# Differential attention with a mixture of experts on one core: the sums of a quad copied by ScalarE, multiplied by GpSimd and transposed once

## The reference, cut to what matters

```
scores = einsum('bhqd,bhkd->bhqk', q, k)
probs = softmax(scores)                       # 32 half heads, in pairs (1, 2)
w = probs[:, :, 0] - lam * probs[:, :, 1]
attn = einsum('bhqk,bhkd->bhqd', w, v)
attn = attn * rsqrt(mean(attn * attn) + EPS) * subln_g
```

## Time and profile before

| what | value |
|---|---|
| median of 3 runs | 6056.91 us (6054.91 to 6063.63) |
| profiled execution | 6064.04 us, span 6062.2 us |
| mean granted TensorE clock | 0.970 |
| PE busy | 5630.7 us (93%) |
| DVE busy | 5537.9 us (91%) |
| ACT busy | 4845.1 us (80%) |
| POOL busy | 2006.0 us (33%) |
| maxima, line 691 | 4096, 4671.1 us busy |
| exponentials, line 677 | 8192, 4368.8 us busy |
| transposes of the sums, line 703 | 256, 179.2 us busy |
| transposes of the output, line 708 | 128, 54.0 us busy |

### The profile page before, as it was taken

The page is one execution under the profiler, slowest core; times in us unless marked ns, Lnnn a source line. Parts: engine busy times, 40 slices in busy tenths (PEclk is TensorE's granted clock), DMA queues, the critical chain, the costliest instruction groups (busy, mean ns, idle before and its releaser), DMA issues. The chain is left out here.

```text
span 6062.2 us, 166095 instructions
## 1 busy us (share of the span) xinstructions
PE 5630.7 (93%) x50896; PEld 2015.1 (33%) x50896; DVE 5537.9 (91%) x6200; ACT 4845.1 (80%) x8950; POOL 2006.0 (33%) x3781
## 2 busy tenths in 40 slices
PE   8878999999999999999999999999999999987775
PEld 4542233333333333333333333333233323325424
DVE  7868999999999999999999999999999999967706
ACT  5755888888888888889888888888888888873304
POOL 7981222222222222222222222222222222225406
PEclk9997999999999999999999999999999999998877
DMA  5672222222232222222222222222222222216598
GB/s 178 203 202 49 49 52 52 51 52 52 52 52 51 52 51 52 51 50 52 52 47 51 52 51 48 51 51 51 50 52 52 52 52 51 52 35 199 173 359 272
DMA packets 436840, 493.13 MB, mean 81 GB/s; under 512 B 99283, under 2 KB 298099, under 8 KB 436195
## 3 DMA queue, kind: packets, MB, share of 16 engines
q1 hardware_dynamic: 435171, 483.57, 32.7%
q10 hardware_dynamic: 1024, 0.53, 0.0%
HBM read 360.60 MB, written 123.21 MB: 80 GB/s over the span
## 5 line engine op out<-in xcount | busy, mean ns | idle before, releaser
L677 ACT ACTIVATE at_e<-at_ps_e 128x512 f32<-128x512 f32 x8192 | 4368.8, 595 | 542.5 <-PE at_ps_e L766 373.2
L691 DVE TENSOR_REDUCE at_largest<-at_ps_m 128x1 f32<-128x1024 f32 x4096 | 4671.1, 1202 | 56.2 <-PE at_ps_m L795 53.0
L782 PE MATMUL at_ps_o<-at_e,at_v 128*32 128x256 f32 (+1 forms) x30720 | 2687.1, 422 | 12.3 <-issue 8.2
L795 PE MATMUL at_ps_m<-k_stack,q_stack 48*128 48x512 bf16 x8192 | 2500.1, 385 | 132.7 <-DVE at_largest L691 58.3
L766 PE MATMUL at_ps_e<-q_stack,k_stack 51*128 51x512 bf16 x8192 | 2505.7, 383 | 5.2 <-issue 2.3
L782 PEld LDWEIGHTS at_ps_o<-at_e,at_v 128*32 128x32 f32 x30720 | 845.0, 149 | 1567.3 <-issue 935.0
L766 PEld LDWEIGHTS at_ps_e<-q_stack,k_stack 51*128 51x128 bf16 x8192 | 598.1, 93 | 1678.3 <-ACT at_e L677 1641.0
L596 POOL TENSOR_TENSOR at_negated<-at_zeros,at_largest_t 128x32 f32<-128x32 f32 x256 | 64.7, 253 | 3262.7 <-DVE at_largest_t L698 3262.7
L795 PEld LDWEIGHTS at_ps_m<-k_stack,q_stack 48*128 48x128 bf16 x8192 | 607.6, 93 | 203.5 <-DVE at_largest L691 172.2
L639 POOL TENSOR_TENSOR at_rms<-at_mean_eps,at_minus_half 128x16 f32<-128x16 f32 x128 | 372.7, 2912 | 10.0
L436 PE MATMUL pr_ps_q<-pr_xn_t,pr_w 128*128 128x512 f32 x512 | 232.3, 596 | 2.0 <-issue 1.3
(11 more groups left out here) (130 smaller groups left out, 2856.0 us busy)
## 6 DMA issues: line engine op xcount, KB each, us to landing
k_stack<-k_parts SPq DMA_DIRECT2D x1536, 64.0 KB
q_stack<-q_parts SPq DMA_DIRECT2D x256, 192.0 KB
q_stack<-q_parts SPq DMA_DIRECT2D x256, 128.0 KB
w_first<-in_w SPq DMA_DIRECT2D x32, 1024.0 KB, 11.7
ex_w_second<-in_w SPq DMA_DIRECT2D x32, 1024.0 KB, 12.7
q_parts<-pr_parts SPq DMA_DIRECT2D x96, 256.0 KB, 2.4
k_parts<-pr_parts SPq DMA_DIRECT2D x96, 256.0 KB, 2.8
pr_x_in<-in_x SPq DMA_DIRECT2D x16, 1024.0 KB, 5.8
```

The source lines that it names most:

```text
L677: nc.scalar.activation(e[:, j % E_BUFS], ps_e[:, bank(u, j)], ACT.Exp, scale=SCALE).then_inc(exp_done, 1)
L691: nc.vector.reduce_max(largest[:, u % 2, j // SIDE, j % SIDE:j % SIDE + 1], ps_m[:, j % 2], AX.X).then_inc(max_done, 1)
L782: last = nc.tensor.matmul(ps_o[32 * tile:32 * tile + 32, columns], v[:, u, tile // 2, kt::TILES], e[:, (QUAD * g + tile) % E_BUFS, columns ...
L795: last = nc.tensor.matmul(ps_m[:, j % 2, half * HALF:(half + 1) * HALF], q_stack[rows, u, pair, c, t * P:(t + 1) * P], k_stack[rows, u, pa ...
```

## The change

The sums no longer go through DVE out of PSUM. ACT copies `ps_o` into SBUF (`sums[:, c]`), and sets `sums_read`. The copy of c stands behind the exponential of position 6 of the following eight periods (`COPY_AT` = 7). The column order of the weights differs between the parts: for c = 0 v first and then ones, for c = 1 ones first and then v. So POOL can multiply the two copies element by element, and the product `crossed` holds V1 s2 in 16 rows and V2 s1 in the other 16. The product s1 s2, needed for EPS, would be spread badly by this; it is made from `totals`, into which SP moves one row of the sums for each of the four head halves and each c, with eight small DMAs for each quad. DVE then transposes both products at once, 544 columns, at g = 5 (`turn_sums`), and the output at g = 11 instead of g = 7 (`turn_out`). `finish` on POOL starts with the two products, waits for the transpose, and then needs fewer steps of its own. The loop of DVE now starts at g = 12.

On SP the order is new: `load_rows` of c = 1, the four totals of c = 1, then `load_stacks`, then `load_rows` of c = 0, `load_v`, the four totals of c = 0, and the store of the quad before.

```
-                        load_rows(n + AHEAD, (u + AHEAD) % BUFS, 1)
...
+                def move_totals(n, c):
+                    sp.wait_ge(sums_read, 2 * n + c + 1 + 1)
+                    sp.sem_inc(passed, 1)
+                    sp.wait_ge(crossed_done, 2 * n + 2)
+                    for g in range(QUAD):
+                        row = 32 * g + (0 if c else VD)
+                        sp.dma_start(totals[32 * g:32 * g + BLOCKS, c], sums[row:row + 1, c]).then_inc(totals_moved, 16)
...
+                    pool.wait_ge(sums_read, 2 * n + 2 + 1)
+                    if not (isinstance(n, int) and n == 0):
+                        pool.wait_ge(sums_turned, n)
+                    nc.gpsimd.tensor_tensor(crossed[:, 0:HALF], sums[:, 0], sums[:, 1], ALU.mult).then_inc(crossed_done, 1)
+                    pool.wait_ge(totals_moved, 16 * TOTAL_DMAS * (n + 1))
+                    nc.gpsimd.tensor_tensor(crossed[:, HALF:], totals[:, 0], totals[:, 1], ALU.mult).then_inc(crossed_done, 1)
+                    pool.wait_ge(sums_turned, n + 1)
...
+                def copy_sums(n, c):
+                    act.wait_ge(sums_done, GROUPS * n + TILES * (c + 1) + E_GROUPS)
+                    act.wait_ge(crossed_done, 2 * n + 2)
+                    nc.scalar.copy(sums[:, c], ps_o[:]).then_inc(sums_read, 1)
+                def turn(n, u, last):
+                    exponentials(n, u, COPY_AT, HALVES // 2 + COPY_AT)
+                    copy_sums(n, 0)
+                    exponentials(n, u, HALVES // 2 + COPY_AT, HALVES)
+                    if not last:
+                        exponentials(n + 1, (u + 1) % BUFS, 0, COPY_AT)
+                    copy_sums(n, 1)
...
-                    nc.vector.transpose(sums_t[:, c].rearrange("p b d -> p (b d)"), ps_o[:]).then_inc(sums_read, 1)
+                    dve.wait_ge(crossed_done, 2 * (n + 1) + 2)
+                    nc.vector.transpose(crossed_t[:], crossed[:]).then_inc(sums_turned, 1)
...
-                    if g == LAG - 1 and last_quad:
-                        turn_sums(n - 1, 1)
-                    if g == HEAD - 1 and last_quad:
+                    if g == TURN_SUMS and last_quad:
+                        turn_sums(n - 1)
+                    if g == TURN_OUT and last_quad:
                         turn_out(n - 1, u - 1)
-                    if g == TILES + LAG - 1 and this_quad:
-                        turn_sums(n, 0)
```

More of the change, by code:

```diff
@@ L492, in attend @@
             parts = sb("parts", [P, PARTS, BLK], BF16)
-            sums_t = sb("sums_t", [P, 2, BLOCKS, BLK])
-            scaled_s1, both = sb("scaled_s1", [P, BLOCKS]), sb("both", [P, BLOCKS])
-            normed, attn_t = sb("normed", [P, 2, BLOCKS, VD]), sb("attn_t", [P, BLOCKS // 2, 2, VD])
+            sums, totals = sb("sums", [P, 2, HALF]), sb("totals", [P, 2, BLK])
+            crossed, crossed_t = sb("crossed", [P, HALF + BLK]), sb("crossed_t", [P, HALF + BLK])
+            second, both = sb("second", [P, BLOCKS, VD]), sb("both", [P, BLOCKS])
+            attn_t = sb("attn_t", [P, BLOCKS // 2, 2, VD])
             attn, square = sb("attn", [P, BLOCKS, VD]), sb("square", [P, BLOCKS, VD])
@@ L560, in store, with first_half, second_half @@
                                      out[32 * g:32 * g + 32, u % 2]).then_inc(out_stored[u % 2], 16)
-                def turn(n, u, load, rows):
-                    if rows:
+                def first_half(n, u, more):
+                    if more:
                         load_rows(n + AHEAD, (u + AHEAD) % BUFS, 0)
                         load_v(n + AHEAD, (u + AHEAD) % BUFS)
+                    move_totals(n, 0)
+                def second_half(n, u, more, load):
+                    if more:
                         load_rows(n + AHEAD, (u + AHEAD) % BUFS, 1)
+                    move_totals(n, 1)
                     if load:
@@ L621, in finish @@
                     pool.wait_ge(pool_step, base + 2)
[L622 to L625, removed]
                     nc.gpsimd.tensor_tensor(both[:], both[:], sixteen_eps[:], ALU.mult).then_inc(pool_step, 1)
-                    pool.wait_ge(pool_step, base + 6)
+                    pool.wait_ge(pool_step, base + 3)
@@ L669, in _, with exponentials @@
                 act.sem_inc(exp_done, SLOTS)
-                with hinted(nc, act, 0, loops + 1, slot=ACT_HEAD) as i:
-                    for u in range(BUFS):
[L672 to L678, removed]
+                act.sem_inc(sums_read, 1)
+                def exponentials(n, u, first, end):
+                    for j in range(first, end):
+                        act.wait_ge(scores_done, HALVES * n + j + 1)
+                        if j % QUAD == 0:
+                            act.wait_ge(sums_done, GROUPS * n + j // QUAD + 1 - E_GROUPS + E_GROUPS)
+                        nc.scalar.activation(e[:, j % E_BUFS], ps_e[:, bank(u, j)], ACT.Exp,
+                                             scale=SCALE).then_inc(exp_done, 1)
+                def copy_sums(n, c):
[9 more added lines that the diff above has]
+                    copy_sums(n, 1)
+                exponentials(0, 0, 0, COPY_AT)
+                with hinted(nc, act, 0, loops, slot=ACT_HEAD) as i:
+                    for u in range(BUFS):
+                        turn(BUFS * i + u, u, False)
+                for u in range(BUFS):
+                    turn(BUFS * loops + u, u, u == BUFS - 1)
             @block.vector
@@ L739, in _ @@
                                         ALU.add).then_inc(lam_done, 1)
-                for g in range(HEAD):
+                for g in range(DVE_HEAD_PERIODS):
                     period(0, 0, g, True, rows=False, last_quad=False)
                 def turn(n, u, tries, next_tries, rows):
-                    for g in range(HEAD, GROUPS):
+                    for g in range(DVE_HEAD_PERIODS, GROUPS):
                         period(n, u, g, tries, rows)
-                    for g in range(HEAD):
+                    for g in range(DVE_HEAD_PERIODS):
                         period(n + 1, u + 1, g, next_tries, rows)
@@ L780, in weighted_sums @@
                         pe.wait_ge(exp_done, HALVES * n + QUAD * (g + 1) + SLOTS)
+                    first = (0 if c else VD * TILES) + kt
                     for tile in range(QUAD):
                         last = nc.tensor.matmul(
-                            ps_o[32 * tile:32 * tile + 32, columns], v[:, u, tile // 2, kt::TILES],
+                            ps_o[32 * tile:32 * tile + 32, columns],
+                            v[:, u, tile // 2, first:first + 2 * VD * TILES - kt:TILES],
                             e[:, (QUAD * g + tile) % E_BUFS, columns],
```

56 lines of the change are left out of this document (33 added, 23 removed).

## The result

The changed kernel takes 6076.35 us (median of 6 runs, 6074.51 to 6088.85) against 6057.44 us before (6 runs, 6054.91 to 6063.63): ratio 1.0033, 95% interval 1.002 to 1.0046. It is slower by 0.33%; the forecast was 6032 us, 25 less than before. The profiled execution of after took 6074.51 us, the lowest of its runs, that of before 6064.04, just above its highest, so the two traces differ by 10.5 us of span where the medians differ by 19. One execution further on, of the kernel before with its branch moved, took 6505.75 us at a granted clock of 0.742 where its neighbours had 0.972 to 0.974, and is left out of its median.

The account below looks back on a forecast made before the run. DVE's chain was taken to bound the kernel, PE close behind. Quads 47 less 17 for loop passes and 4.6 for the end gave 25 us less: 6039 profiled, 6032 as median; range 6018 to 6046 (0.63).

Parts of the forecast that it names:

- What bounds the kernel: In attention, DVE's own chain of maxima and transposes sets the quad of 37.90 us, with PE close behind (1.137 against 1.131).
- DVE's gain of 0.57 a quad: On DVE, two 512-column transposes (1.20 us) give way to one of 544 (0.63): at most 73 us over 127 intervals.
- The idle where a part begins: At each boundary DVE idles 0.08 us without the transpose; with PE's slower pace 0.20 a quad, leaving 47 us gain.
- the lead's floor: Shortest time from the start of PE's second attempt matmul to the start of the DVE maximum reading it: 0.41 us.
- first rival: PE catches up between DVE's transposes, so DVE never idles: 68 us less at most, 5989 us; chance 0.17.
- The copy on ACT costs nothing: ACT's copy of the sums releases PE in time in ordinary quads, with a margin of 0.1 us: no cost.
- Totals and POOL are in time for DVE: SP's totals and POOL's product are ready 1.6 us before DVE's transpose; POOL's output about 3029 against 3034.7: no cost.
- Loop passes, 17 us: At PE's loop branch, g = 8, a smaller lead and late copy lose 0.56 us in each of 31 passes.
- The stacks start 1.7 us later and are needed a whole quad later. All of this costs nothing: On SP, the totals' issues delay the stack loads by 1.7 us, claimed to cost nothing.
- 50 us, which may differ by 10: The stalls at PE's loop branch come to some 50 us over 31 passes, with 10 us of variation allowed.
- The end: In the last quad nothing hides `finish`: 3.6 us more, plus 1 for ACT's two copies, 4.6 us in all.

## Why the prediction was wrong

- *What bounds the kernel; DVE's gain of 0.57 a quad*: right. The 544 wide transpose pushes the next maximum by 0.66 (taken: 0.65).
- *The idle where a part begins*: right in kind, too small. It is 0.106, then 0.011 more, instead of 0.08, since the lead's floor while DVE trails PE is 0.44, not the 0.41 that I read behind a stall. The runs that move transposes show it: cover one boundary, 37.49; both, 37.32. The ordinary quad is 37.65 (median) instead of 37.53; the gain is 32 us, not 47. (A slip besides: 127 x 0.57 is 72, not 73; only the first rival's time rests on it, by 1 us.)
- *The copy on ACT costs nothing*: right; its margin is 0.16.
- *Totals and POOL are in time for DVE*: right. `crossed` is ready 1.6 us ahead of DVE in the median, as forecast, the output 5.85 ahead.
- *Loop passes, 17 us*: right for what it priced. Short passes lose 0.5 us each (0.56 forecast).
- ***"The stacks start 1.7 us later and are needed a whole quad later. All of this costs nothing"*: this step failed**, and with it the bound "50 us, which may differ by 10". I asked who needs the stacks and not who else moves data meanwhile. They start 2.9 us later (each total takes 0.59 to issue, 0.63 apart, and there is a wait ahead), and in about every fourth pass the instruction packet that PE needs at g = 8 comes late while they are in flight: 36 us more in the long passes. The run without totals and the one without totals at g = 14 show no other cost of the totals. I also read one pass for all, though 50 us over 31 passes is 1.6 us each and that row shows 0.98: the mean said that other passes were longer.
- *The end*: from the last maximum to `route` 58.0 us instead of 54.0: 4.0, forecast 4.6.

On the profiled runs: start -1, quads -32, passes +44 (the intervals without a branch give 2 of the 46 back), end +4, stages behind -4: together +11, span +10.5. The forecast was -25, so the traces explain 36 of the 44 us by which the time came out above it: 15 in the quads, 27 in the passes, less 6 at the start, the end and behind. The other 8 lie between the profiled executions and the medians, and no trace shows them.

The first rival (PE catches up, 5989) fell: where DVE trails PE its distance in after is 1.138 us, and behind a boundary it gains nothing back. So the rule of the Trainium skill's "TensorEngine Tiling (Array Packing)", Key Properties, on draining at a change of tiling mode, is the one that this trace agrees with; no run changed the tiling, so that a drain makes the 1.138 isn't shown.

Open: why long stalls grew even without totals, by 17 us in the traces and less by the medians. Some 5 of it is the smaller lead, as in the short passes, and some 5 is the tenth long stall; the rest wasn't separated. Open too is why only every fourth pass is long, though the stacks are loaded in every quad. In the run with the branch at g = 14 each fourth pass still differs: one packet earlier, the start is 6.0 to 10.3 us ahead of PE's stop there and 10.7 to 12.5 in the others, but PE doesn't stand for it. That the instruction packet queues behind q1's packets on its DMA engine is the likely mechanism, but the runs show only that the stalls go with the loads in flight and last as long as the packet is late.

## What to carry to other kernels

A transfer that nobody waits for is not free if an engine's loop branch falls among its packets: look at what moves when each engine branches, and put the branch where the queues are quiet (here one constant was worth 21 us in the kernel before and 69 in the kernel after). Take loop passes from the whole set, not from one. A transpose on DVE placed just ahead of a hold-up of PE hides it; elsewhere the same transpose gives a lead that nobody uses.

## What was not expected of the hardware

A long stall also costs the clock. By windows, before the stall, in it and behind it:

```profile
3140.00:3145.00 5.00, 4.62 (x48) 1.53 (x47) 4.94 (x5) 3.99 (x9) 4.53 (x9) 1.00 0.68 105
...
3150.00:3155.00 5.00, 1.99 (x13) 0.35 (x12) 1.22 (x1) 0.00 (x0) 0.00 (x0) 0.50 0.23 35
3155.00:3160.00 5.00, 4.66 (x38) 1.19 (x36) 3.73 (x4) 4.04 (x8) 0.00 (x0) 0.83 0.10 29
3160.00:3165.00 5.00, 5.00 (x58) 1.54 (x52) 5.00 (x6) 4.76 (x10) 0.00 (x0) 1.00 0.03 8
```

After 7.4 us without a matmul the granted clock is 0.50, which is 1.2 GHz, and eight matmuls take 1.09 us instead of 0.67; DVE idles 0.79, 0.40 and 0.22 more behind its 7.73. From the stall on, the maxima of this quad lose 1.6 us against an ordinary quad, those behind the short stall at 3457.2 lose 0.3. Behind a stall of 0.98 us the matmuls stay at 0.38, full speed. So this long stall costs some 1.3 us on top of its length, an estimate from the two losses.
